# A fused tokenizer, attention and gelu kernel: offset rows by one transfer, a split last group, later preparation, constant products

## The chip, the cores and the metric

The program runs on one core of one Trainium2 chip. The metric is the device time in microseconds of one execution. The core has TensorE (matrix products; it loads the stationary operand first, which the profile counts as PEld), VectorE (DVE), ScalarE (ACT), GpSimd (POOL) and SyncE (SP), which here issues every transfer. Each engine works through its own list of instructions in order; semaphores connect the lists.

## The reference, cut to what matters

Input are 64 images of 3 x 84 x 84 and 64 texts of 77 rows of 192. For each image:

1. Stem: a 4 x 4 convolution with stride 4 to 96 channels on 21 x 21 pixels, batch norm, leaky ReLU.
2. Deformable convolution: a 4 x 4, stride 4 convolution gives 32 offsets (y and x for 16 taps) at 25 positions. Every tap is read bilinearly at its shifted place (zero outside), which makes 96 x 16 values a position; they are multiplied with a 192 x 1536 weight, then bias, batch norm, leaky ReLU: 25 tokens of 192.
3. The 25 tokens and the 77 text rows make 102 rows of 192.
4. Attention: layer norm, integer-rounded q, k, v for 12 heads of 16, scores rounded to 8 bits, an integer softmax (floor, a polynomial for the exponential, a power of two as the result), the weighted sum of v, an output projection, all rounded, plus the residual.
5. Gelu layer: layer norm, 192 to 768 with bias, gelu, 768 to 192, plus the residual. Output is 64 x 102 x 192 in fp32.

## The kernel before, in words

Images are worked in groups of four (GRP), 16 groups in all. The work of a group is cut into named stages, and `SLOT` (lines 66 to 96) is one list of `engine.stage.lag`: in round s the stage works on image s - lag, or, for the stages in `PER_GROUP`, on the whole group. `walk` (line 173) lays the rounds one behind the other, so the order in which an engine meets its stages is written out by hand and repeats each group; up to five groups are under way at a time. `BANKS` (line 101) says which of six PSUM banks a stage's product goes to, and `BankUse` (line 111) makes TensorE wait until the last product of that bank has been read.

The stages that matter here:

- STEM (L1073): the stem as one product for each image; ScalarE's leaky ReLU writes H (L586). HTT (L1081): H transposed in four pieces, copied to HT by ScalarE (L594).
- OFF (L1097), OFS (L1104): the offsets, in four quarters of the partitions, then their sum by `fold`, three copies below one another. ScalarE adds the bias (L609). OFS on GpSimd (`split_offsets`, L523 to L533) splits them into three bf16 parts that sum to the fp32 value, 96 rows in OFFS.
- RX on GpSimd (`mask_offsets`, L544), once an image: the 96 rows are multiplied with a mask that keeps each offset only in the columns of its own tap; with three constant rows this is the right operand, 99 rows of 400 columns (16 taps x 25 positions).
- HAT on TensorE (L1113, L1115): two products with constant lines, the distance of every pixel of a strip from every sampling place in x and y. ScalarE takes absolute values (L618, L622), VectorE turns them into hat functions (HAT, L852) and multiplies x with y (HATW, L858). INT (L1125 to L1129): the interpolation as a product of HT with these weights, copied by ScalarE to SAMP (L629). SD: three transfers pack 96 channels x 16 taps into 128 rows x 12.
- DCN (L1141, L1143): the token product of a group. ScalarE's leaky ReLU writes TOKB (L636); SP stores it (line 481) and loads it back beside the text (LA, line 433).
- LS1, LN1, VE1, RS1, LN1X: statistics, variance, inverse root (GpSimd, L562) and normalised rows XH (L892); TensorE transposes them (L1153), ScalarE copies them to XT (L641). V and FQ: v and q, k. QKC: casts on VectorE (L907 to L911). QD: twelve transfers place the queries of the heads (line 460). SC: scores (L1208, L1211), scaled by ScalarE (L680), clipped by VectorE (L917).
- MAX, MXB, MXC: the row maximum on VectorE (L924 to L934); MAX on GpSimd: the distance from it (L554). BND, QQ, QQG, REM, EP, EXP, SUM, RCP: the integer exponential and its sum on VectorE (L940 to L989); SQ, LOG, PR on ScalarE: square, ten logarithms (L694) and the ratio (L702). PW, PR on VectorE: the power of two (L999, L1006). PT: a transposing transfer. PV2, PV3: weighted sum of v and projection (L1222, L1232). RES: residual (L1025).
- LS2, LN2, VE2, RS2, LN2X: the second layer norm, the same way, into XT2. FFN0, FFN1, FFN2 (`rows_192`, L1174, L1178): two of the six 128-row blocks of the gelu layer each, 408 columns for four images; ScalarE's gelu writes GE (L718), between two loads of its function tables (L572). FF2 (L1247): an image's output product, all in bank 2; VectorE adds the residual (L1032) and frees the bank. YO: two stores a group.
- PREP0 to PREP3: weight preparation on VectorE, once, on the first group: batch norm folded into the tap weights WD (L768 to L772), scalars and rounded qkv weights (L776 to L817, L824, L825), projection weights (L829 to L843). `sampling_constants` (L755) comes before all of them.

What sets the order around the change: before, on VectorE PREP0 and PREP1 stand in front of the first HAT, PREP2 and PREP3 behind the last HATW; on TensorE a steady round runs OFS, FFN0 to FFN2, DCN, HAT 0, FF2 0, FF2 1, HAT 1, FF2 2, PV2, STEM0, LN1X 0, FF2 3, LN1X 1, PV3, LN1X 2, PV2, LN1X 3, V0, FQ0 and so on, with one HTT of the round behind it.

## Time and profile before

| | |
|---|---|
| Runs, median (lowest to highest) | 1056.89 us (1053.66 to 1061.37), 3 runs |
| The profiled execution | 1055.49 us, span from first to last instruction 1053.7 us |
| Busy: TensorE, weight loads | 885.7 us (84%), 539.3 us (51%) |
| Busy: VectorE, ScalarE, GpSimd | 883.3 us (84%), 793.0 us (75%), 301.2 us (29%) |
| Mean granted TensorE clock | 0.950 of full speed |
| Transfers | 53.23 MB, 51 GB/s over the span |

How to read it: busy times are unions, so two instructions that overlap count once. An engine's idle time in front of an instruction is put down to what ended it ("<-"), where that can be inferred. 2.4 GHz is TensorE's full clock; the throttle may grant half of it. The chain of waits that ended last changes engines every microsecond or two; no line of it has over 1.4% of the span beside 4.7% of "issue".

### The profile page before, as it was taken

What the parts mean: (1) busy time and instruction counts of PE and PEld (TensorE: products, weight loads), DVE (VectorE), ACT (ScalarE), POOL (GpSimd) and SP (SyncE); (2) the same over time, 40 slices, a digit from 0 to 9 for tenths busy, and PEclk for the clock granted to TensorE, in tenths of its full rate; (3) what the DMA queues carried; (4) which work ended last, traced back from release to release, by engine and by line L of the source; (5) the groups of instructions that cost most, each with busy time, mean ns of one, the idle gap of its engine ahead of it and who ended that gap; (6) DMA issues with size and microseconds to landing.
All of it is one profiled execution on the core that took longest, in us unless ns stands there. A gap on an engine that the chain in (4) does not pass through costs nothing. (4 is left out here: it accounts for less than half of the span.)

```text
span 1053.7 us, 18633 instructions
## 1 busy us (share of the span) xinstructions
PE 885.7 (84%) x5570; PEld 539.3 (51%) x5570; DVE 883.3 (84%) x1887; ACT 793.0 (75%) x1841; POOL 301.2 (29%) x243
## 2 busy tenths in 40 slices
PE   3769489898989899898989898998989897876737
PEld 2335345555555555555465555555555656454424
DVE  3956988989899898989898998989898989985850
ACT  1435777969697978879696979889796969675742
POOL 5020506042241505051332415050513324130300
PEclk9978779999999999999999999999999999996768
DMA  6010221313122222313121212223141312123020
GB/s 171 22 34 7 59 44 44 63 34 70 41 57 33 65 50 55 60 33 79 37 65 40 64 32 65 50 54 61 33 79 36 65 34 56 32 52 68 11 52 12
DMA packets 131342, 53.23 MB, mean 51 GB/s; under 512 B 103814, under 2 KB 130124, under 8 KB 131148
## 3 DMA queue, kind: packets, MB, share of 16 engines
q1 hardware_dynamic: 131244, 52.05, 23.0%
q8 instruction: 46, 0.75, 0.3%
q14 instruction: 52, 0.43, 0.1%
HBM read 19.84 MB, written 6.24 MB: 25 GB/s over the span
## 5 line engine op out<-in xcount | busy, mean ns | idle before, releaser
L554 POOL TENSOR_TENSOR m_sb<-mx_sb,a_sb 128x1020 f16<-128x1020 f16 x64 | 147.5, 2305 | 192.1 <-DVE mx_sb L934 192.1
L694 ACT ACTIVATE ee_sb<-ee_sb,rs_sb 128x102 f32<-128x102 f32 x640 | 180.1, 379 | 2.8 <-DVE rs_sb L989 2.5
L1247 PE MATMUL bank<-w_out_sb,ge_sb 128*102 128x192 f32 x768 | 144.6, 340 | 37.9 <-DVE y_sb L1032 30.0
L562 POOL TENSOR_TENSOR rstd_sb<-ve_sb,half_sb 102x4 f32<-102x4 f32 x32 | 34.5, 1080 | 445.7 <-DVE ve_sb L885 445.7
L1247 PEld LDWEIGHTS bank<-w_out_sb,ge_sb 128*102 128x102 f32 x768 | 125.8, 175 | 55.0 <-issue 50.3
L1129 PE MATMUL bank<-hats_sb,ht_sb 127*96 127x400 f32 (+1 forms) x384 | 145.1, 514 | 5.4 <-DVE hats_sb L858 5.4
L858 DVE TENSOR_TENSOR hats_sb<-hats_sb 126x1600 f32<-126x1600 f32 x64 | 116.0, 1813 | 0.2
L622 ACT ACTIVATE hats_sb<-bank 126x400 f32<-126x400 f32 (+1 forms) x256 | 107.5, 510 | 0.4 <-PE bank L1115 0.3
L680 ACT ACTIVATE a_sb<-scores,sc_sb 128x1020 f16<-128x1020 f32 x64 | 71.0, 1110 | 39.4 <-POOL m_sb L554 29.7
L1129 PEld LDWEIGHTS bank<-hats_sb,ht_sb 127*96 127x96 f32 (+1 forms) x384 | 59.1, 164 | 72.8 <-issue 64.3
L1174 PE MATMUL bank<-xt_sb,w_in_sb 128*128 128x408 f32 x192 | 84.7, 553 | 8.3 <-ACT ge_sb L718 7.6
L544 POOL TENSOR_TENSOR rx_sb<-offs_sb,mask_sb 96x400 bf16<-96x400 bf16 x64 | 78.8, 1241 | 42.0 <-PE bank L1115 40.6
L1153 PE MATMUL bank<-ident_sb,xh_sb 102*128 102x102 f32 x256 | 51.5, 286 | 46.6 <-ACT xt_sb L641 23.5
L976 DVE SCALAR_TENSOR_TENSOR ee_sb<-sq_sb,sc_sb,ep_sb 128x1020 f32<-128x1020 f32 x64 | 83.3, 1302 | 2.4 <-ACT sq_sb L687 1.2
L641 ACT ACTIVATE xt_sb<-bank 128x204 f32<-128x204 f32 x128 | 43.3, 338 | 49.7 <-PE bank L1153 48.3
L687 ACT ACTIVATE sq_sb<-rm_sb,sc_sb 128x1020 f32<-128x1020 f16 x64 | 73.8, 1154 | 7.0 <-DVE rm_sb L961 7.0
L984 DVE TENSOR_REDUCE ss_sb<-ee_sb 128x10 f32<-128x1020 f32 x64 | 77.2, 1206 | 0.0
L852 DVE TENSOR_SCALAR hats_sb<-hats_sb 126x2000 f32<-126x2000 f32 x64 | 76.5, 1196 | 0.7 <-ACT hats_sb L622 0.7
L1153 PEld LDWEIGHTS bank<-ident_sb,xh_sb 102*128 102x128 f32 x256 | 28.4, 149 | 82.4 <-DVE xh_sb L892 66.2
L1143 PE MATMUL bank<-wdcn_sb,samp_sb 128*100 128x192 f32 x384 | 69.6, 340 | 0.0
L702 ACT ACTIVATE rr_sb<-ee_sb 128x1020 uint16<-128x1020 f32 x64 | 67.2, 1051 | 0.6
L1143 PEld LDWEIGHTS bank<-wdcn_sb,samp_sb 128*100 128x100 f32 x384 | 63.9, 174 | 4.6 <-issue 4.0
(165 smaller groups left out, 1794.9 us busy)
## 6 DMA issues: line engine op xcount, KB each, us to landing
xc_sb<-x_col SPq DMA_DIRECT2D x32, 165.4 KB, 3.1
out<-y_sb SPq DMA_DIRECT2D x32, 153.0 KB
xa_sb<-txt SPq DMA_DIRECT2D x16, 231.0 KB
xr_sb<-txt SPq DMA_DIRECT2D x16, 231.0 KB
q_sb<-qb_sb SPq DMA_DIRECT2D x192, 12.8 KB, 1.9
samp_sb<-samp_sb SPq DMA_DIRECT2D x48, 50.0 KB, 1.9
tok_scratch<-tokb_sb SPq DMA_DIRECT2D x16, 75.0 KB
xa_sb<-tok_scratch SPq DMA_DIRECT2D x16, 75.0 KB
```

Source lines behind the costliest of these rows:

```text
L544: nc.gpsimd.tensor_tensor(RX[b][0:3 * NOFF, :, :], OFFS[:, t.i, :].unsqueeze(1).to_broadcast([3 * NOFF, TAPS, POS]), mask[:].unsqueeze(2). ...
L554: nc.gpsimd.tensor_tensor(M16[b][:], MX[b][:].unsqueeze(2).to_broadcast([128, RT, TOK]), A16[b][:], ALU.subtract).then_inc(m_done, 1)
L622: nc.scalar.activation(HATS[t.i][0:rows, 1 + j, :], bank[t.banks[1]][0:rows, 0:SMP], ACT.Abs, bias=float(-line)).then_inc(ay_done, 1)
L694: last = nc.scalar.activation(EE[b][:, r, :], EE[b][:, r, :], ACT.Ln, scale=RS[b][:, r:r + 1])
L858: v.tensor_tensor(hat[:, 1:, :], hat[:, 1:, :], hat[:, 0:1, :].to_broadcast([rows, NCH, SMP]), ALU.mult).then_inc(w_done, 1)
L976: v.scalar_tensor_tensor(EE[b][:].rearrange("p h k -> p (h k)"), SQ[:], sc[:, CC:CC + 1], EP[:].bitcast(bf16), ALU.add, ALU.mult).then_inc ...
L984: v.tensor_reduce(SS[b][:], EE[b][:], AX.X, ALU.add).then_inc(ss_done, 1)
L1129: last = mm(dst, HT[0:rows, t.i, j, :], HATS[t.i][0:rows, 1 + j, :], start=(j == 0 and not odd), stop=(j == NCH - 2 and odd == 1))
L1143: last = mm(dst, SAMP[:, k, :, :].rearrange("c g p -> c (g p)"), WD[:, k, :], start=False, stop=(k == PACKED - 1))
L1153: last = nc.tensor.transpose(bank[t.banks[0]][:, c * TOK:(c + 1) * TOK], xh[b][:, 64 * c:64 * c + 128], ident[0:TOK, 0:TOK])
L1174: mm(bank[t.banks[c]][:, 0:GRP * TOK], weights(k + c, c), src[:, c, :], start=True, stop=False)
L1247: last = mm(bank[t.banks[0]][0:TOK, 0:D], GE[:, f, t.i * TOK:(t.i + 1) * TOK], WOUT[:, f, :], start=(f == 0), stop=(f == FT - 1))
```

## The change

- Offset rows: RX becomes 9 rows x 16 taps x 4 images x 25 positions, two of them for two groups. Three rows are constant, the six others are the parts of y and x; one transfer of SP a group (`spread_offsets`, stage RP) lays the 96 rows of OFFS into them, tap beside tap. The masks, their constants and `mask_offsets` go. `fold`'s columns are reordered for it, by a copy on VectorE.
- Preparation: PREP1 to PREP3 now stand behind the first group's HAT and HATW on VectorE; the multiplication of the tap weights goes from PREP0 to GpSimd (WDF), behind its first split. The four scalar loads count to the later group of loads.
- Last group: FFA makes the six blocks for the first two images (204 columns each, four banks), FFN0 to FFN2 those for the other two. Moments, variance and inverse root of that group come in pairs too (LN2A, RS2A). Gelu's tables are loaded twice.
- Constant products: `warm` multiplies a constant square with itself, 18 times before and 12 times after the first product; KW00 to KW04 (group 0) and KW10 to KW12 (last group) are four squares each at set places of TensorE's order.
- The whole of SLOT is new, and so are most BANKS. Lags of one engine count from another zero than before, which has no meaning in itself. TensorE's round now runs OFF, LN2X 3, FFA, SC 3, FFN0, OFS, FFN1, FFN2, DCN, HAT 0, FF2 0, FF2 1, HAT 1, PV2 0, STEM0, FF2 2, LN1X 0, HTT 3, PV3 0, LN1X 1, FF2 3, LN1X 2, PV2 1, LN1X 3, V0, FQ0, FQ1, STEM1, HAT 2, INT 0, PV2 2, PV3 1, HTT 0, HAT 3, INT 1, PV3, PV2, INT 2, HTT 1, PV3, SC 0, INT 3, SC 1, LN2X 0, V1, HTT 2, LN2X 1, SC 2, LN2X 2.

```diff
-BANKS = dict(STEM0=(3, 5), STEM1=(1, 4), HTT=(3,), OFF=(3,), OFS=(2,), HAT=(4, 5), INT=(2, 4),
-             DCN=(2,), LN1X=(4,), LN2X=(1,), V0=(0, 3), V1=(5, 0), FQ0=(4, 1), FQ1=(2, 5), PV2=(1,),
-             PV3=(0,), FFN0=(1, 5), FFN1=(4, 3), FFN2=(0, 5), FF2=(2,))
+BANKS = dict(KW00=(1,), KW01=(4,), KW02=(0,), KW03=(1,), KW04=(1,), KW10=(4,), KW11=(4,), KW12=(0,),
+             FFA=(5, 2, 1, 0), STEM0=(3, 2), STEM1=(1, 4), HTT=(4,), OFF=(5,), OFS=(2,), HAT=(5, 0),
+             INT=(3, 1), DCN=(5,), LN1X=(3,), LN2X=(2,), V0=(0, 2), V1=(3, 5), FQ0=(3, 4),
+             FQ1=(0, 5), PV2=(5,), PV3=(0,), FFN0=(1, 5), FFN1=(4, 3), FFN2=(0, 2), FF2=(1,))
...
+            def spread_offsets(t):
+
+                b = t.n % 2
+                sp.wait_ge(part_s, t.count(4, 4))
+                if t.n >= 2:
+                    sp.wait_ge(dy_full, t.count(GRP, -GRP))
+                sp.dma_start(RX[b][3:OFF_ROWS, :, :, :].rearrange("r k g p -> r k (g p)"),
+                             OFFS[:].rearrange("o g p -> o (g p)")).then_inc(rx_in, 16)
...
+            def fold_taps(t):
+                if t.n < 1:
+                    pool.wait_ge(prep, BN2_STEPS)
+                    nc.gpsimd.tensor_tensor(WD[:], WD[:], inv2.unsqueeze(1).to_broadcast([128, PACKED, D]),
+                                            ALU.mult).then_inc(wd_ready, 1)
...
-            def mask_offsets(t):
-
-                b = t.i % 2
...
-                nc.gpsimd.tensor_tensor(RX[b][0:3 * NOFF, :, :],
-                                        OFFS[:, t.i, :].unsqueeze(1).to_broadcast([3 * NOFF, TAPS, POS]),
-                                        mask[:].unsqueeze(2).to_broadcast([3 * NOFF, TAPS, POS]),
-                                        ALU.mult).then_inc(rx_done, 1)
...
+            def warm(dst, square, count):
+
+                for _ in range(count):
+                    last = mm(dst[:, 0:128], square[:], square[:], start=True, stop=True)
+                return last
...
+            warm(bank[1], onesq, 18)
             pe.wait_ge(diag_s, 1)
...
+            warm(bank[1], onesq, 12)
             pe.wait_ge(prep, W1_STEPS)
...
+            def keep_clock(t, end, k):
+
+                if t.n == (LAST_GROUP if end else 0):
+                    free.take(t, 0, warm_s[end][k], 0, 0)
+                    warm(bank[t.banks[0]], ident, 4).then_inc(warm_s[end][k], 1)
...
-                pe.wait_ge(rx_done, t.count(1, 1))
-                rhs = RX[b][:].rearrange("o k p -> o (k p)")
+                pe.wait_ge(rx_in, t.of_group(16, 16))
+                rhs = RX[t.n // GRP % 2][:, :, t.i, :]
...
+            def ffn_in_first_pair(t):
+
+                if t.n == LAST_GROUP:
+                    pe.wait_ge(xt2_done, t.count(GRP, 2))
+                    for f in range(0, FT, 2):
+                        rows_192(t, f, w_in_of, XT2[:, :, 0:2, :].rearrange("p c g q -> p c (g q)"),
+                                 f1_full, ge_done, f % 4)
...
             def ffn_out(t):
-                pe.wait_ge(ge_done, t.of_group(6, 6))
+                pe.wait_ge(ge_done, t.of_group(6, 12 if t.n >= IMG - 2 else 6))
```

## Rows read from the trace of the kernel before

**Rows 1.** Busy us (count) of each engine in a stretch, granted clock, transfers:
```profile
527.00:585.00 58.00, 52.84 (x351) 32.48 (x350) 53.40 (x115) 49.25 (x116) 18.49 (x15) 1.00 0.24 53
```
**Rows 2.** Timeline of VectorE: start us, length us, engine, line, operation, idle before:
```profile
533.93 0.36 DVE L1032 TENSOR_TENSOR y_sb<-bank,x_sb 102x192 f32<-102x192 f32 x1 [0.76 <-PE bank L1247]
...
591.77 0.36 DVE L1032 TENSOR_TENSOR y_sb<-bank,x_sb 102x192 f32<-102x192 f32 x1 [0.76 <-PE bank L1247]
```
**Rows 3.** Waits of TensorE from 411 to 643: us in total, times, longest:
```profile
PE bank L1247 <- DVE y_sb L1032: 6.8, 8, 1.2
PE bank L1153 <- ACT xt_sb L641: 6.4, 12, 0.7
...
PE bank L1174 <- ACT ge_sb L718: 2.2, 4, 0.8
```
**Rows 4.** Timeline of TensorE around the output products:
```profile
582.12 0.95 PE L1174 MATMUL bank<-xt_sb,w_in_sb 128*128 128x408 f32 x2 [0.67 <-ACT ge_sb L718]
...
589.56 2.17 PE L1247 MATMUL bank<-w_out_sb,ge_sb 128*102 128x192 f32 x12 [0.34 <-ACT tokb_sb L636]
592.27 2.17 PE L1247 MATMUL bank<-w_out_sb,ge_sb 128*102 128x192 f32 x12 [0.54 <-DVE y_sb L1032]
...
595.95 2.17 PE L1247 MATMUL bank<-w_out_sb,ge_sb 128*102 128x192 f32 x12 [1.17 <-DVE y_sb L1032]
...
598.36 1.77 PE L1073 MATMUL bank<-xc_sb,stem_w_sb 49*96 49x441 f32 x4
600.65 0.39 PE L1153 MATMUL bank<-ident_sb,xh_sb 102*128 102x102 f32 x2 [0.53 <-DVE xh_sb L892]
...
603.67 0.36 PE L1153 MATMUL bank<-ident_sb,xh_sb 102*128 102x102 f32 x2 [0.67 <-ACT xt_sb L641]
```
**Rows 5.** Waits of VectorE from 411 to 643:
```profile
DVE m_sb L940 <- POOL m_sb L554: 7.1, 4, 1.8
```
**Rows 6.** Single lines over the whole run: count, duration in ns (min/median/max):
```profile
L544 POOL TENSOR_TENSOR rx_sb<-offs_sb,mask_sb x64: 848/1297/1727, 25.2 to 884.7; 96x400 bf16<-96x400 bf16 x64
...
L917 DVE TENSOR_SCALAR a_sb<-a_sb x64: 411/428/1747, 99.5 to 983.9; 128x1020 f16<-128x1020 f16 x64
...
L523 POOL TENSOR_TENSOR offp_sb<-offt_sb,later_sb x16: 350/398/2648, 21.0 to 874.4; 96x100 bf16<-96x100 f32 x16
```
**Rows 7.** Timeline of ScalarE, the logarithms in front of the token copy:
```profile
528.56 2.81 ACT L694 ACTIVATE ee_sb<-ee_sb,rs_sb 128x102 f32<-128x102 f32 x10
```
**Rows 8.** Transfers by line: count, KB each, median us from issue to landing:
```profile
q_sb<-qb_sb SPq DMA_DIRECT2D x192, 12.8 KB, 1.9
```
**Rows 9.** Busy us of each engine in two stretches of the start:
```profile
24.80:37.00 12.20, 7.31 (x14) 2.62 (x14) 11.12 (x32) 7.72 (x18) 3.60 (x5) 1.00 0.29 97
37.00:49.80 12.80, 9.45 (x31) 4.62 (x31) 11.97 (x10) 3.94 (x10) 0.00 (x0) 1.00 0.00 1
```
**Rows 10.** Timeline of the start, all engines:
```profile
26.13 0.56 PE L1113 MATMUL bank<-rx_sb,lx_sb 99*126 99x400 bf16 x1 [5.60 <-DVE sc_sb L782]
...
27.13 1.69 ACT L622 ACTIVATE hats_sb<-bank 126x400 f32<-126x400 f32 x4
...
29.39 0.39 PEld L1073 LDWEIGHTS bank<-xc_sb,stem_w_sb 49*96 49x96 f32 x2 [0.34 <-DMA xc_sb<-x_col]
...
37.05 1.20 DVE L852 TENSOR_SCALAR hats_sb<-hats_sb 126x2000 f32<-126x2000 f32 x1
...
40.17 4.14 PE L1129 MATMUL bank<-hats_sb,ht_sb 126*96 126x400 f32 x6 [5.38 <-DVE hats_sb L858]
...
46.02 2.26 PE L1129 MATMUL bank<-hats_sb,ht_sb 127*96 127x400 f32 x6
...
72.19 1.14 DVE L871 BATCH_NORM_STATS2 st_sb<-xa_sb 102x6 f32<-102x192 f32 x4 [10.13 <-DMA xa_sb<-tok_scratch]
```
**Rows 11.** Timeline of the end:
```profile
1022.28 1.01 POOL L562 TENSOR_TENSOR rstd_sb<-ve_sb,half_sb 102x4 f32<-102x4 f32 x1 [26.80 <-DVE ve_sb L885]
...
1039.60 2.20 PE L1247 MATMUL bank<-w_out_sb,ge_sb 128*102 128x192 f32 x12 [1.18 <-ACT ge_sb L718]
```

215 lines of the change are left out of this document (129 added, 86 removed).

## The prediction

> **What bounds the kernel now.** I read first the busy time of a steady stretch [rows 1]: in 58 us TensorE is busy 52.84, VectorE 53.40, ScalarE 49.25, GpSimd 18.49. No engine is full, two are close to it, so the time is made of busy time plus waits between engines. One group of four images takes the distance of two equal instructions: VectorE's first output addition stands at 533.93 and 591.77 [rows 2], 57.84 apart. Sixteen groups make some 925 of the 1053.7 us; the rest is the way in and the way out.
>
> Which engine closes the period is read from the idle time in front of TensorE's instructions [rows 3, 4]. Over four periods TensorE waited 6.8 us for additions that free the last product's bank, 6.4 for ScalarE to copy transposes, 2.2 for gelu to free a bank; with 0.53 a period for normalised rows, 0.34 for ScalarE's copy of the tokens and some 0.2 of other it is 5.0 a period: 52.84 + 5.0 = 57.84, exactly the period. These waits lie in one short stretch, from the end of the token product to the projection of v (589 to 606); from there TensorE runs without a break until gelu's 0.67 at 582. So the loop is: TensorE's long stretch, then an exchange FF2, addition, normalisation, transpose with VectorE. VectorE has 4.4 us of slack in a period; its largest wait, 1.8 a period for the distance from the maximum [rows 5], costs time only where it makes an addition late.
>
> **Offset rows by transfer.** GpSimd loses the four mask multiplications of a group, 1.30 us each by the median [rows 6], 5.2 us. GpSimd is 32% busy, so its own time is worth nothing. What it does to others is seen in VectorE's clip: 0.428 us by the median, 1.747 at worst [rows 6]. GpSimd stood beside the long ones. The Trainium skill, "GPSIMD Engine Reference", section "Key points", says that GpSimd shares its memory interfaces with VectorE and contends with its two-port modes and its two-input instructions; the spread of the clip agrees. By it GpSimd's remaining work, which is the larger part, still contends. I count 1 us of VectorE's time a period as freed, nothing of it directly on TensorE's loop; bounds 0 and 1.4. One transfer of 19 KB (96 rows of 100 values of 2 bytes) replaces the masks. Transfers of 12.8 KB took 1.9 us [rows 8]; the new one starts after GpSimd's split and is wanted only behind FFN1, FFN2 and DCN, over 8 us of TensorE's work, so it is hidden. Its place on SP is behind the patch loads, queries, packed samples and residual loads; behind it wait the token store and the loads that feed the first layer norm. It waits for the split, which ends before the token product does, so it holds up nobody: cost 0. The two distance products read 9 rows instead of 99; their columns stay 400, so I take no change.
>
> **The new order and banks.** This touches every period, and I price it by the waits of [rows 4]:
> - FF2: the second product still stands right behind the first: 0.54 stays. The third now stands behind the second's hats product, PV2 and the stem (1.77), so the 1.17 goes. The fourth stands after LN1X of image 1, and on VectorE its predecessor's addition after two normalisations, EP and REM: a new wait of 0.7. Sum 1.2 where 1.7 was.
> - Transposes: LN1X of image 0 comes a product later (0.53 becomes 0); images 1 and 2 have HTT, PV3 or FF2 in front of them (0.67 each becomes 0.1), image 3 keeps 0.4. Sum 0.6 where 2.2 was.
> - gelu: FFN2 uses banks 0 and 2, not 5, which FFN0 had: 0.55 becomes 0.
> - Tokens: DCN and the first hats product now share bank 5. Before, the hats product covered part of the wait of 0.34 in front of FF2; now it waits itself: 0.9.
> - Other: three interpolations come before the scores and need VectorE's weights sooner: 0.5 where 0.2 was.
> Sum 3.2, period 52.84 + 3.2 = 56.0; every order leaves some coincidence that such a sum does not see, and I take 56.4: 1.4 us gained, 15 times, **21 us**. Bounds: all waits come back elsewhere (57.84, nothing), or only the 0.54, the 0.9 and half of the rest stay (55.2, 40 us).
>
> **The start.** VectorE's first hats wait behind the scalar and weight preparation (11.12 busy in 24.8 to 37) until 37.05; then hats (to 49.8), then the remaining preparation (to 62.06, where 10.13 us of idling for the tokens begin) until 72.19 [rows 9, 10]. Now the hats come first. But the preparation is not gone: 12.8 of hats and 12.2 + 12.2 of preparation make 37.2 in a row before the first layer norm. They start when the offset rows have landed and a hat is made of them, 2.7 us from the first distance product (26.13) to ScalarE's last of four (27.13 and 1.69) [rows 10]. Without the long split step and the mask (2.3 and 0.85) the rows would be split at about 23; I allow up to 24, for three transposes now ahead of the offset products. The transfer takes 1.9, or it stands behind the weight loads, behind which the second patches became usable only at 29.39 [rows 10]. That gives 27.6 to 32 for the first hat and 65 to 69 for the layer norm, plus up to 3 for stems that ScalarE does before the third hat. I take 70: **2 us gained**, bounds 0 and 6. The token product, 9 us earlier, gains nothing alone: VectorE is late in its place. The tap weights' multiplication moves to GpSimd: 2304 columns by the 0.848 for 400 are 4.9 us, behind the first split, 20 us ahead of DCN: 0; and the split's first step no longer runs beside it (2.648 at worst, 0.398 by the median [rows 6]), which the chain gets back and the transfer spends.
>
> **Constant products.** A fp32 product of 400 columns took 0.69 us per instruction at 40 and 0.377 at 46 [rows 10]; the granted clock in between rose to 2.4 GHz. A 128-column square is thus 0.44 or 0.24 us, 18 of them 7.9 or 4.3, before the first real product, which was due at 5.6. They delay it by 0 to 3.5 and may halve the first stems (1.8 us each): 0 in sum, bounds -2 and +3. The Trainium skill, "TensorE: Matmul & The Clock Gate", section "The HAM clock gate", says that sustained work brings the full rate and idling takes it back. By it the squares help the stems only, since the wait for the first offsets is not filled. The steady stretch is at full clock already [rows 1]. Of the eight groups of four squares three stand among full periods: 1 us each, of which I take **2 us lost**.
>
> **The end.** The last group's chain went VectorE, GpSimd 1.01 at 1022.28, normalisation, transposes, FFN, last gelu, 1.18 us of TensorE idle, FF2 at 1039.60 [rows 11]. Statistics of the first pair are now ready earlier, but its transposes and its FFN stand behind the second pair's on VectorE and TensorE; so what is saved is the wait for gelu (1.18) and part of the 1.01 for GpSimd. Four squares between the first two transposes cost 1 to 1.8. Two more table loads lie under TensorE's products. **1 us gained**, bounds -3 and +4.
>
> **Sum.** 1055.5 (the profiled execution: span 1053.7 and 1.8 around it; 1.4 below the median of 1056.9) - 21 - 2 + 2 - 1 = 1033.5. I forecast **1034**.
>
> **Rivals.**
> 1. *Waits all go* (chance 0.18). TensorE's period is 55.2: 1055.5 - 40 - 1 = about 1015. For it: VectorE has slack of 4 us and GpSimd is freed. Against: FF2 and additions still alternate on one bank.
> 2. *Waits only move* (0.19). The new order gives each wait a new owner, period 57.6 to 57.9; start, end and squares leave 1050 to 1055. For it: both busy engines leave under 5 us a period, and the old order had reached that too. Here the change does at the ends what it says and nothing in the middle.
> 3. *Slower: the token copy* (0.10). DCN and the next hats product share bank 5, and ScalarE's copy of the tokens stands behind ten logarithms, 2.81 us [rows 7], that need VectorE's reciprocal. If these start only when DCN ends, TensorE waits 3.1 instead of 0.34: period 56.4 + 2.2 = 58.6, +0.8 x 15, about 1068 with the ends. It decides from a wait of 2.3 us. Against: the old order has the same logarithms in front of the same copy, and TensorE waited 0.34 for it [rows 4].
> 4. *Forecast* (0.53): 1034, from 1022 to 1044.
>
> **The numbers.** The range takes the forecast, half of rival 1 and most of rival 2: 1016 to 1053. Within 1% is what a measurement of this kernel can hardly tell from no change, 1046.3 to 1067.5. Faster by over 1%: 0.53 + 0.18 + 0.02 of rival 2 = 0.73. Same: 0.18. Slower: 0.09, where rival 3 goes past its price.
>
> **What would show it.** Distance of equal additions: 56.4, not 57.8. No idle of 1.2 before the third FF2, 0.7 before the fourth; bank 5 wait under 1.5 before the hats product. GpSimd busy 230 us, VectorE's clip as before in the worst case. First layer norm near 70, with VectorE busy right up to it. If the additions are 57.8 apart with other waits, rival 2; if ScalarE's token copy is named in front of the hats product with over 2 us, rival 3. The forecast is wrong most easily in the 1.4 us a period.

## The result, and the profile after

| | before | changed |
|---|---|---|
| Median of 18 runs (lowest to highest) | 1057.14 us (1053.33 to 1064.6) | 1063.74 us (1054.45 to 1070.61) |
| Ratio, changed to before | | 1.0049, 95% interval 1.0029 to 1.007 |
| Profiled execution (its span) | 1055.49 (1053.7) us | 1057.11 (1055.3) us |
| Busy, whole run: TensorE, VectorE, ScalarE, GpSimd | 885.7, 883.3, 793.0, 301.2 us | 896.0, 906.5, 798.3, 217.6 us |
| First y addition of group 0, of group 13, of group 15, end | 183.8, 939.8, 1041.8, 1053.7 | 181.6, 944.4, 1043.4, 1055.3 |

The change makes the kernel half a per cent slower; 1034 was forecast. The last row of the table, taken from VectorE's additions (L1032 before, L1084 now), says where: 2.2 us gained before the first of them, 6.8 lost in the 13 periods that follow, 3.0 gained in the last two, 1.6 lost in sum. The 21 us expected of the middle are missing altogether. The profiled execution of the changed kernel is among its fastest, 6.6 us under its median, that of the kernel before 1.65 under its own; so the two traces show 1.6 us of a loss of 5 (by the ratio) to 6.6 us (by the medians).

The steady stretch again, busy time by engine as in [rows 1], here in three neighbouring stretches of the changed kernel:

```profile
469.00:527.00 58.00, 53.31 (x351) 33.84 (x350) 54.85 (x113) 49.23 (x116) 12.71 (x10) 0.97 0.27 53
527.00:585.00 58.00, 51.48 (x350) 32.29 (x349) 55.02 (x115) 49.35 (x117) 12.72 (x10) 1.00 0.27 53
585.00:643.00 58.00, 53.32 (x351) 33.79 (x350) 54.91 (x114) 49.40 (x117) 12.72 (x10) 0.97 0.29 53
```

GpSimd fell from 18.49 to 12.7, as forecast. VectorE was to lose 1 us of its 53.40 and gained 1.6. TensorE reads 51.48 at full clock and 53.3 where the clock fell for a moment, and yet the additions stand 57.8 to 58.1 apart in all three: TensorE's amount of work does not set the distance. At full clock it is also less than before, by 1.2 us over one period, first the kernel before, then the changed one:

```profile
533.93:591.77 57.84, 52.67 (x348) 32.32 (x348) 53.23 (x114) 49.09 (x116) 18.33 (x15) 1.00 0.24 52
534.04:591.87 57.83, 51.46 (x348) 32.28 (x348) 54.76 (x114) 49.19 (x116) 12.72 (x10) 1.00 0.27 52
```

So TensorE idles 6.4 us in that period where it idled 5.2.

The additions that answer to [rows 2], VectorE's timeline:

```profile
534.04 0.36 DVE L1084 TENSOR_TENSOR y_sb<-bank,x_sb 102x192 f32<-102x192 f32 x1 [0.87 <-DMA out<-y_sb]
...
591.87 0.36 DVE L1084 TENSOR_TENSOR y_sb<-bank,x_sb 102x192 f32<-102x192 f32 x1 [1.05 <-DMA out<-y_sb]
```

57.83 apart, where 57.84 was. What ended the wait in front of them is new: not TensorE, but the store of the output rows of the group before. All waits of TensorE and VectorE over the four periods from 411 to 643, answering to [rows 3] and [rows 5] (us in total, times, longest):

```profile
PE bank L1332 <- DVE y_sb L1084: 8.5, 4, 2.2
PE bank L1184 <- ACT tokb_sb L660: 4.2, 4, 1.1
DVE y_sb L1084 <- DMA out<-y_sb: 4.1, 4, 1.2
PE bank L1295 <- DMA pt_sb<-p_sb: 3.9, 4, 1.2
PE bank L1225 <- ACT xt_sb L665: 3.2, 5, 1.8
```

TensorE's waits are 2.1 + 1.05 + 1.0 + 0.8 and 0.05 of others a period: 5.0, the same sum as before, under other names. That is a mean over four periods: 6.2 where the clock stays full, 4.4 to 4.9 where it falls. The wait for gelu and the one of 1.17 before the third output product are gone, as forecast. In their place stand one of 2.1 before the second output product and one of 1.0 for the transposed probabilities, of which the forecast knew nothing.

Why the store is late is seen on SyncE. Timeline around one exchange, several engines:

```profile
582.25 0.83 SPq L492 DMA_DIRECT2D rx_sb<-offs_sb  x1
...
584.43 2.81 ACT L718 ACTIVATE ee_sb<-ee_sb,rs_sb 128x102 f32<-128x102 f32 x10
...
587.15 0.31 ACT L660 ACTIVATE tokb_sb<-bank 100x192 f32<-100x192 f32 x1
587.49 0.29 SPq L498 DMA_DIRECT2D tok_scratch<-tokb_sb  x1
...
587.83 0.30 SPq L504 DMA_DIRECT2D out<-y_sb  x1
...
592.37 2.17 PE L1332 MATMUL bank<-w_out_sb,ge_sb 128*102 128x192 f32 x12 [2.09 <-DVE y_sb L1084]
```

The first output store of a group (L504) has had its rows since the exchange of the period before. In the new order it stands on SyncE behind the token store (L498), which waits for ScalarE's copy (L660), behind ten logarithms. It is issued at 587.83; only when it has landed may VectorE overwrite the rows, at 591.87, some 4 us later, and TensorE's second output product waits 2.09 for that. In the kernel before, the same store left right behind the exchange, 47 us ahead of the addition at 591.77:

```profile
544.46 0.60 SPq L487 DMA_DIRECT2D out<-y_sb  x1
```

VectorE's own growth sits in two lines. Count and duration in ns (min/median/max) over the run, answering to [rows 6], and GpSimd's distance from the maximum:

```profile
L969 DVE TENSOR_SCALAR a_sb<-a_sb x64: 414/421/2051, 101.3 to 990.8; 128x1020 f16<-128x1020 f16 x64
...
L1020 DVE TENSOR_SCALAR ep_sb<-qq_sb x64: 413/421/2119, 107.9 to 1007.5; 128x1020 int16<-128x1020 int16 x64
...
L564 POOL TENSOR_TENSOR m_sb<-mx_sb,a_sb x64: 1884/1891/2937, 103.1 to 1002.5; 128x1020 f16<-128x1020 f16 x64
```

The clip (L969) and the power bits (L1020) take 0.42 alone. Three times a period one of them starts beside GpSimd's distance of 1.89 and takes 1.8 to 2.1 (over the run 25 clips of 64 take 0.97 or more, with a median of 2.04, and 15 power bits of 64 take 2.1).

The start, answering to [rows 10]; timeline of GpSimd, SyncE, TensorE and VectorE:

```profile
23.44 0.37 POOL L556 TENSOR_TENSOR offs_sb<-offr_sb,offp_sb 96x100 bf16<-96x100 f32 x1
...
23.84 0.86 SPq L492 DMA_DIRECT2D rx_sb<-offs_sb  x1
...
30.25 0.56 PE L1184 MATMUL bank<-rx_sb,lx_sb 9*126 9x400 bf16 x1 [7.71 <-issue]
...
33.07 1.20 DVE L891 TENSOR_SCALAR hats_sb<-hats_sb 126x2000 f32<-126x2000 f32 x1 [9.05 <-ACT hats_sb L646]
...
72.76 1.14 DVE L922 BATCH_NORM_STATS2 st_sb<-xa_sb 102x6 f32<-102x192 f32 x4
```

The rows were split at 23.81 and of use at 30.25: 6.4 us for a transfer priced at 1.9, while the weight and patch loads of the start were under way (333 GB/s from 22.5 to 27.7, 281 to 30.2). VectorE idles 9.05 for the first hats, and the first layer norm starts at 72.76, 0.57 later than before, now without a wait in front of it.

### The profile page after: what moved, and what is told of

It reads as the page before. It is cut to its first block and busy times, and to the rows that moved or that the text cites. A ratio compares the mean times of both kernels' runs of the same rounds, so it can differ in the third digit from the quotient of the medians.

```text
span 1055.3 us, 18850 instructions
## 1 busy us (share of the span) xinstructions
PE 896.0 (85%) x5718; PEld 566.4 (54%) x5718; DVE 906.5 (86%) x1887; ACT 798.3 (76%) x1849; POOL 217.6 (21%) x181
## 5 line engine op out<-in xcount | busy, mean ns | idle before, releaser
L1332 PE MATMUL bank<-w_out_sb,ge_sb 128*102 128x192 f32 x768 | 155.4, 357 | 38.4 <-DVE y_sb L1084 37.2
L564 POOL TENSOR_TENSOR m_sb<-mx_sb,a_sb 128x1020 f16<-128x1020 f16 x64 | 128.3, 2005 | 267.1 <-DVE mx_sb L986 267.1
L718 ACT ACTIVATE ee_sb<-ee_sb,rs_sb 128x102 f32<-128x102 f32 x640 | 180.1, 378 | 1.6 <-DVE rs_sb L1041 1.2
L1332 PEld LDWEIGHTS bank<-w_out_sb,ge_sb 128*102 128x102 f32 x768 | 132.9, 184 | 60.5 <-issue 56.0
L573 POOL TENSOR_TENSOR rstd_sb<-ve_sb,half_sb 102x4 f32<-102x4 f32 (+1 forms) x33 | 38.1, 1154 | 455.4 <-DVE ve_sb L937 455.4
L1200 PEld LDWEIGHTS bank<-hats_sb,ht_sb 127*96 127x96 f32 (+1 forms) x384 | 58.2, 164 | 71.5 <-issue 69.4
L1028 DVE SCALAR_TENSOR_TENSOR ee_sb<-sq_sb,sc_sb,ep_sb 128x1020 f32<-128x1020 f32 x64 | 81.6, 1275 | 4.0 <-ACT sq_sb L711 2.3
L1247 PE MATMUL bank<-xt_sb,w_in_sb 128*128 128x408 f32 (+1 forms) x204 | 82.7, 530 | 0.0
L969 DVE TENSOR_SCALAR a_sb<-a_sb 128x1020 f16<-128x1020 f16 x64 | 61.9, 968 | 13.3 <-ACT a_sb L704 13.2
L665 ACT ACTIVATE xt_sb<-bank 128x204 f32<-128x204 f32 x128 | 43.7, 342 | 36.5 <-PE bank L1225 36.3
L740 ACT ACTIVATE ge_sb<-bank,b_in_sb 128x408 f32<-128x408 f32 (+1 forms) x102 | 53.4, 577 | 11.9 <-PE bank L1251 10.9
## 6 DMA issues: line engine op xcount, KB each, us to landing
q_sb<-qb_sb SPq DMA_DIRECT2D x192, 12.8 KB, 1.9
```

The costliest lines, as they stand in the source:

```text
L564: nc.gpsimd.tensor_tensor(M16[b][:], MX[b][:].unsqueeze(2).to_broadcast([128, RT, TOK]), A16[b][:], ALU.subtract).then_inc(m_done, 1)
L718: last = nc.scalar.activation(EE[b][:, r, :], EE[b][:, r, :], ACT.Ln, scale=RS[b][:, r:r + 1])
L1028: v.scalar_tensor_tensor(EE[b][:].rearrange("p h k -> p (h k)"), SQ[:], sc[:, CC:CC + 1], EP[:].bitcast(bf16), ALU.add, ALU.mult).then_inc ...
L1200: last = mm(dst, HT[0:rows, t.i, j, :], HATS[t.i][0:rows, 1 + j, :], start=(j == 0 and not odd), stop=(j == NCH - 2 and odd == 1))
L1247: mm(bank[t.banks[first + c]][:, 0:n], weights(k + c, c), src[:, c, :], start=True, stop=False)
L1332: last = mm(bank[t.banks[0]][0:TOK, 0:D], GE[:, f, t.i * TOK:(t.i + 1) * TOK], WOUT[:, f, :], start=(f == 0), stop=(f == FT - 1))
```

## The experiments

All ratios are to the kernel before, on the same chip. "Store-first" is the changed kernel with the mend of the first experiment.

**e1_store_first.** Edit, in the list of the order:

```diff
-dve.PREP0.0 ... act.SQ.12 dve.HATW.92 sp.DCN.8
+dve.PREP0.0 ... act.SQ.12 dve.HATW.92
-dve.SC.99 ... sp.YO0.20 dve.MAX.99 ...
+dve.SC.99 ... sp.YO0.20 sp.DCN.8 dve.MAX.99 ...
```

> The changed kernel with one entry moved: SyncE issues the first output store of a group (YO0) ahead of the store of the tokens (DCN), not behind it. In the changed kernel VectorE's first output addition waits 0.9 to 1.05 us in each group for that store, which is issued at 587.8 though its rows are ready 57 us earlier, and TensorE's second output product waits 2.2 us behind it. Theory A, SyncE's queue closes the loop: both waits fall (the first to 0, the second to about 1.2), the distance of equal additions goes from 58.0 to about 57.0, and the time is about 15 us under that of the changed kernel, near 1049 (ratio to the kernel before about 0.992). Theory B, VectorE (busy 55.0 of 58.0, with short waits of many kinds) and ScalarE close it: the wait for the store goes, another wait of VectorE or TensorE takes its place, the distance stays 57.7 to 58.1, and the ratio to the kernel before stays at 1.002 to 1.007.

Measured: 1042.27 us, ratio 0.9884 (0.9846 to 0.9922), intervals apart from the changed kernel's. VectorE's additions, no wait left in front of them, 56.73 apart (57.0 to 57.4 in most periods):

```profile
526.70 0.35 DVE L1084 TENSOR_TENSOR y_sb<-bank,x_sb 102x192 f32<-102x192 f32 x1
...
583.43 0.35 DVE L1084 TENSOR_TENSOR y_sb<-bank,x_sb 102x192 f32<-102x192 f32 x1
```

Theory A holds, and the gain is larger than its 0.992, which still lies inside the interval: one entry in SyncE's queue cost 1.65%, more than the whole change lost. The steady period fell by about 0.8 us, which makes 12 us of the 17; the two traces differ by 15.1 over the 13 periods, since long ones are fewer too.

**e2_old_order.** The changed code with the order and the banks of before, the last group in one piece, no constant products; the list against that of before:

```diff
-... pool.RX.5 ... pool.RX.4 ... pool.OFS.0 ... pool.RX.3 ... sp.LR.12 ... pool.RX.2 ...
+... pool.OFS.0 pool.WDF.0 ... sp.LR.12 sp.RP.4 ...
```

> The offset rows by one transfer a group and the tap weights' product on GpSimd, but the order of all engines and the banks of the kernel before, the last group in one piece and no constant products. Theory A, the new order brought nothing and the transfer nothing: within 0.2% of the kernel before, period 57.8 to 58.0, VectorE's clip as before. Theory B, GpSimd freed of the masks makes VectorE faster, as forecast: VectorE busy 52.4 a period where 53.4 was, period up to 1 us less, 1042 to 1050. Theory C, GpSimd's distance from the maximum, once it no longer waits behind masks, stands beside VectorE's two-port operations: VectorE busy 54.5 to 55 a period, period 58.2 or more, ratio 1.003 to 1.010. In the changed kernel VectorE's busy time of a period rose from 53.4 to 55.0; A and B put that on the new order, C on the masks' going.

Measured: 1060.31 us, 1.0051 (1.002 to 1.0082). Busy time by engine in the steady stretch:

```profile
527.00:585.00 58.00, 53.26 (x350) 32.25 (x348) 52.62 (x115) 49.19 (x116) 13.32 (x11) 1.00 0.25 53
```

A new wait of TensorE, over four periods:

```profile
PE bank L1176 <- DMA rx_sb<-offs_sb: 3.4, 4, 0.9
```

VectorE is at 51.9 to 52.7 in five neighbouring stretches, 53.0 to 53.4 before, so the masks' going did free some 0.9 of the 1 us forecast, and theory C falls: it is the new order that put VectorE up. The time did not follow: the steady period stayed at 57.9, with 0.85 for the landing of the rows in the place of older waits. Nor does the steady period show the half per cent that this kernel is slower; in its trace the first addition comes 3.0 us later than before, and one late period takes 62.3.

**e8_old_order_split_first.** In e2's list `pool.OFS.0` moved ahead of `pool.MAX.9`.

> The old order with the transfer (ratio 1.005), and GpSimd's split of the offsets ahead of the distance of the third image, not behind it. There the rows are split at 531.2 and land at about 534, TensorE waits 0.88 for them before the first hats product of each group, though ScalarE's offsets are ready at 524.06. Theory E, the transfer's latency is what the old order pays: the wait goes, period 57.0, ratio 0.992 to 0.995. Theory F, in the old order the waits only move (the loop is closed elsewhere): wait gone, period still 57.8, ratio 1.000 to 1.006. If so, transfer and masks are worth nothing by themselves.

Measured: 1064.51 us, 1.0065 (1.0041 to 1.009). The wait for the rows is gone, TensorE waits 0.6 for the token copy and as long as before for transposes instead, and the steady period is 57.9: theory F. In the old order this wait only moved.

**e3_no_squares.** All constant products taken out.

```diff
-            warm(bank[1], onesq, 18)
-            warm(bank[1], onesq, 12)
-WARM = 5, 3
+WARM = 0, 0
```

> The changed kernel without any of its constant products (the 30 at the start and the 8 groups of four). By the forecast's step they cost 2 us: about 1062, 0.998 of the changed kernel. If they cost nothing that ends last: the same as the changed kernel within 1 us. Rival, they are worth something: the first stems and the products before the first offset rows take 2 to 3 us longer at the lower clock, first normalised rows later than 75.7, and the time is 2 to 4 us above the changed kernel (ratio to the kernel before 1.007 to 1.009).

Measured: 1056.93 us, 1.0018 (0.9995 to 1.0042), some 3 us less than with them by the ratios; the intervals overlap, so that it is clear neither of nothing nor of the forecast's 2. The products do halve the stems (0.98 for the first pair, 1.79 before), but these start 2.3 us later behind them (9.11 without), and the offset sum 1.6 later (19.72 without). The first addition stands only 0.6 us earlier without them, so where the rest of the 3 us lies is not shown. TensorE's timeline of the changed kernel:

```profile
11.44 0.98 PE L1136 MATMUL bank<-xc_sb,stem_w_sb 49*96 49x441 f32 x4
...
21.29 0.34 PE L1175 MATMUL bank<-offq_sb,fold_sb 128*96 128x100 f32 x2
```

**e4_one_piece.** The conditions on the last group set to never true for the layer norm and gelu layer (`PAIRS = -1`).

> The changed kernel with the last group's second layer norm and gelu layer in one piece, as before (four images, no FFA). By the forecast's step the split is worth 1 us: about 1064.7. Theory of this run: from the last group's first output addition to the end the changed kernel takes 11.9 us (1043.4 to 1055.3) and the kernel before 11.9 (1041.8 to 1053.7), but the distance of the last two first additions fell from 45.9 to 42.8, and if that is the split, then without it the end comes 3 us later: 1066 to 1067. Rival: the split costs, by its second pair of table loads (1.28 us each) and its narrower products, and without it the time is 1 to 2 us lower.

Measured: 1064.39 us, 1.0086 (1.0054 to 1.0119). By the ratios the split is worth 0.37%, some 4 us, but the intervals overlap, and 1 us is not ruled out. In the traces the last two distances between first additions sum to 102.3 in one piece, 99.0 split, 102.0 before; among the other kernels with the split that sum goes from 98.0 (e3) to 104.9 (e1), so one trace does not settle it either.

**e5_distance_on_vector.** On store-first:

```diff
-                nc.gpsimd.tensor_tensor(M16[b][:], MX[b][:].unsqueeze(2).to_broadcast([128, RT, TOK]),
+                v.tensor_tensor(M16[b][:], MX[b][:].unsqueeze(2).to_broadcast([128, RT, TOK]),
                                 A16[b][:], ALU.subtract).then_inc(m_done, 1)
```

> The store-first kernel with the distance from the maximum computed by VectorE, right behind the last maximum, and no more by GpSimd. In the store-first kernel VectorE is busy 55 to 55.7 us in 58; its clip of 0.43 takes 1.77 and 2.06, its power bits 2.11 instead of 0.42, each time next to GpSimd's distance of 1.9, some 4.9 us a period over the shortest durations. Theory C, the two engines are in each other's way, and VectorE is now the bound: the four distances cost VectorE 4 x 0.69 = 2.8 (the row of the remainder, same kind and size) and the clip and power bits are back at 0.42 in every instance; VectorE busy about 2 us less a period, the waits for GpSimd go, period 55 to 56.3 where 57.1 was, ratio to the kernel before 0.955 to 0.977. Theory D, the long ones are not GpSimd's doing (their place, or their data, makes them long): they stay, VectorE gets 2.8 us more, period 58.5 or more, ratio over 1.005.

Measured: 1059.22 us, 1.0037 (1.0019 to 1.0056). The clip over the whole run of this kernel, and then VectorE's groups by shape from 411 to 643 (busy, mean ns, idle before):

```profile
L962 DVE TENSOR_SCALAR a_sb<-a_sb x64: 364/421/536, 100.0 to 991.5; 128x1020 f16<-128x1020 f16 x64
```

```profile
L986 DVE TENSOR_TENSOR m_sb<-mx_sb,a_sb 128x1020 f16<-128x1020 f16 x16 | 19.5, 1221 | 0.5
...
L1021 DVE TENSOR_SCALAR ep_sb<-qq_sb 128x1020 int16<-128x1020 int16 x16 | 6.7, 419 | 0.0
```

The mechanism of theory C is shown: with no distance on GpSimd, no clip takes over 0.54 and the power bits 0.42 on average. The price of theory C was wrong: the distance costs VectorE 1.22, not 0.69, since one operand is broadcast. Four of them are 4.9 us, as much as the interference had cost: VectorE is busy 55.1 us a period here and 54.7 in e1. In VectorE's time GpSimd's help with the distance is worth next to nothing. In the kernel's time it is worth 1.5%: the period is 58.5, where e1 has 57.0 to 57.4. What VectorE's 0.4 us do not explain of that is not shown.

**e6_sums_behind, e11_maxima_behind_exp, e12_both.** VectorE's softmax in other orders, on store-first. e6: `MXC1 EXP0 SUM0 RCP0 SC2 ... MXC2 EXP1 SUM1 RCP1 SC3`. e11: `SC2 MAX2 EXP0 MXC1 SUM0 RCP0 ... SC3 MAX3 EXP1 MXC2 SUM1 RCP1`, and ScalarE's SC3 behind FFN1, SQ1 behind FFN2. e12: e11 with DCN in bank 4.

> The store-first kernel with VectorE's order changed within the softmax: remainder and power bits of images 0 and 1 ahead of the next image's last maximum, and exponential, sum and reciprocal behind it, ahead of the next clip; so an fp32 exponential (1.28) and sum (1.21) stand beside GpSimd's distance of images 1 and 2 (1.9 each), not a 16-bit clip or power bits. Theory C, 16-bit one-input operations wait for GpSimd and these do not: two of the three long instances of a period (1.6 too long each) go back to 0.42, VectorE busy about 3 us less a period, period 56 or a little under if no wait takes their place, ratio 0.965 to 0.98. Theory D, what stands beside GpSimd is slowed whatever it is: VectorE's busy time as in the store-first kernel, ratio 0.986 to 0.992. Third outcome: exponentials now wait for ScalarE's square, VectorE less busy but more idle, ratio 0.985 or above.

> The store-first kernel with VectorE's softmax in another order: the last maxima of images 1 and 2, which release GpSimd's distance, stand behind the exponential of the image before, so that the sum (1.21, a reduction) stands beside the distance, as it already does in the last image, where neither is slowed. The ordering tried before put the exponential beside it, and that took 10.4 us too long in four periods. ScalarE's scaling of the fourth scores goes behind FFN1's gelu and its second square behind FFN2's, since the distance comes some 4 us later. Theory C: clip and power bits of images 1 and 2 are back at 0.42, the clip of image 1 stays long; VectorE's busy time of a period falls from 54.8 to 51.5 to 52.5, period 55.5 to 56.5, ratio 0.964 to 0.98. Rival: VectorE is less busy, but its softmax now waits for ScalarE's squares and GpSimd's distance in a row, period 57 to 59, ratio 0.987 to 1.01.

> Both changes of the two kernels before it: token product in bank 4, last maxima behind the exponential. If theory C holds (VectorE busy 2.5 us less) and TensorE's exchange is the next in line, the bank gives another 0.5 to 1 us a period over the new softmax order alone: 0.955 to 0.97. If the bank is worth nothing in either order, the same as the new softmax order within 0.2%.

Measured: 1090.24 us, 1.0301 (1.0275 to 1.0326); 1083.26 us, 1.0244 (1.0212 to 1.0276); 1094.34 us, 1.0336 (1.0295 to 1.0377). In e6 the exponential, which theory C had keep its time, was the one held up (31 of 64, 2.5 by the median), L1028 over the run:

```profile
L1028 DVE SCALAR_TENSOR_TENSOR ee_sb<-sq_sb,sc_sb,ep_sb x64: 1270/1282/2833, 108.6 to 1045.8; 128x1020 f32<-128x1020 f32 x64
```

In e11 VectorE was less busy (51.4 to 53.4 in 58), but waited 9.6 us in four periods for ScalarE's squares and TensorE 8.3 for the token copy, and periods of 58.6 and 60.6 took turns: the rival. In e11 longer waits in the chain cost more than the interference did. The token bank on top (e12) made it slower again, not faster.

**e7_store_first_no_squares.**

> The store-first kernel without any constant products. In the order of the changed kernel they cost about 3 us (ratio 1.0018 without, 1.0049 with). If they delay the start alone, the same is saved here: ratio 0.985 to 0.987. If the saving was in the period through TensorE's clock, it is saved or not whatever the order: the granted clock of the run then is above 0.94.

Measured: 1042.35 us, 0.9868 (0.9839 to 0.9898). It lies under e1's 0.9884 by half of what e3 saved, but within the intervals; not told apart. The granted clock is higher, 0.938 to 0.949 where e1 has 0.927 to 0.939, but most of that is no gain: the trace of e1 counts 17 us at half rate ahead of 43.7, that of e7 has no entry of the clock ahead of 43.4 and counts that time as full.

**e9_prep_first, e14_scalars_first.** On e7. e9: `dve.PREP1.92` back to `dve.PREP1.0`, behind PREP0. e14:

```diff
                 then(v.tensor_tensor(dcnb[:], dcnb[:], bm2[:, 0, :], ALU.add))
+                scalars()
...
             def qkv_integers():
-                scalars()
```

> The store-first kernel without constant products (ratio 0.9868), and the scalars and the rounding of the qkv weights (PREP1) back in front of VectorE's first hats, where they stood before; the projection weights stay behind the hats. In the changed kernel VectorE idles 9.05 us at 33.07 for the first hats (the offset rows, split at 23.81, reach TensorE at 30.22, 6.4 us later, not 1.9), then 22.6 us of preparation follow the hats and the first layer norm starts at 72.76, with VectorE busy up to it. Theory G, this idle time is what the new place of the preparation wasted: with 12.2 us of it ahead of the hats these start near 37, the preparation behind them is 10 us shorter, first layer norm at 64 to 69 (or when the tokens have landed), everything after it 4 to 8 us earlier, ratio 0.979 to 0.983. Rival: the tokens now land near 72 as before (the token product and its round trip close the start), VectorE idles there instead, ratio 0.985 to 0.989.

> The store-first kernel without constant products, and of the preparation only the scalars (5.9 us of small operations, 50.18 to 56.03 in the changed kernel) in front of the first hats, where VectorE idles 9.05; all the rest stays behind them. With the whole preparation behind the hats VectorE reaches the first layer norm at 72.76 and the tokens (issued 66.15) have long landed; with PREP1 in front the hats start near 37 and the tokens land at 72.2. Theory: both ends count, and this takes 5.9 off VectorE's and nothing from the tokens': first layer norm when the tokens land, 69.4 to 70, 3 us earlier, ratio 0.983 to 0.985. Rival: the 3 us are lost again before the second group (q and k, low granted clock of TensorE from 67 to 84), ratio 0.986 to 0.988.

Measured: e9 1043.48 us, 0.9866 (0.983 to 0.9902), its rival; e14 1039.13 us, 0.9825 (0.9784 to 0.9866), as its theory has it, though its interval overlaps that of e7. VectorE's first layer norm in e9:

```profile
72.20 1.14 DVE L921 BATCH_NORM_STATS2 st_sb<-xa_sb 102x6 f32<-102x192 f32 x4 [8.51 <-DMA xa_sb<-tok_scratch]
```

and in e14:

```profile
69.71 1.14 DVE L921 BATCH_NORM_STATS2 st_sb<-xa_sb 102x6 f32<-102x192 f32 x4 [2.55 <-DMA xa_sb<-tok_scratch]
```

Two ends close the start: VectorE's preparation and the landing of the tokens. All of the preparation behind the hats makes VectorE the later one (72.76), 12 us of it in front makes the tokens late (72.20, 8.51 idle). The 5.9 us that fit in the idle time bring the first layer norm 3 us forward, as expected, and the first addition of group 0 stands at 177.4, after 180.3 in e7. That second number scatters: it is 175.4 to 180.1 in the four kernels with the scalars first, 180.0 to 182.2 in e1, e7 and e15 without.

**e10_token_bank.** On store-first, `DCN=(5,)` to `DCN=(4,)`.

> The store-first kernel with the token product in bank 4 and not in bank 5, which it shares with the next hats product. There TensorE waits 1.11 in each group for ScalarE's copy of the tokens, behind ten logarithms (rival 3 of the prediction). Theory H, TensorE's exchange closes the loop of 57.1: the wait goes, the period falls to 56.0 to 56.4, ratio 0.972 to 0.978. Theory I, VectorE (54.8 busy of 57.1) closes it: the wait goes and comes back in front of the second output product and the transposes, period 57.0 to 57.3, ratio 0.986 to 0.990.

Measured: 1051.06 us, 0.9926 (0.9898 to 0.9955), slower than store-first if anything. TensorE's waits over four periods:

```profile
PE bank L1332 <- DVE y_sb L1084: 7.6, 4, 2.4
PE bank L1295 <- DMA pt_sb<-p_sb: 4.5, 3, 2.1
```

The wait for the token copy is gone and the one before the second output product is back (1.9 a period for store-first's 1.0). Periods of 57.1 to 57.9 and of 58.3 to 58.5 take turns. Neither theory had it slower.

**e13_no_clip.** On e7, the clip left out, the first maximum waiting for the scores themselves.

> The store-first kernel without constant products (ratio 0.9868), with VectorE's clip of the scores left out, nothing else (so out-of-range scores are not limited; what is computed differs in that). The four clips take 0.42, 1.77, 0.41 and 2.06 of VectorE in a period, 4.7 in sum; part of the two long ones will pass to whatever then stands beside GpSimd's distance. Theory I, VectorE closes the loop of 57.1: the period falls by at least the four short ones, 1.7, to 53.5 to 55.4, ratio 0.93 to 0.962. Theory H', TensorE (52.2 to 52.6 busy) or ScalarE (50.3) closes it by its exchanges: the period stays above 56.5, ratio 0.978 or more.

Measured: 1042.44 us, 0.9845 (0.9793 to 0.9897), period 57.0 to 57.2. Busy time in the steady stretch, and then VectorE's greatest wait over four periods:

```profile
527.00:585.00 58.00, 53.37 (x350) 33.69 (x348) 52.88 (x110) 50.05 (x119) 13.19 (x11) 0.97 0.27 54
```

```profile
DVE m_sb L990 <- POOL m_sb L563: 7.4, 4, 1.9
```

Theory I falls: VectorE does 2.8 us less in 58 (55.7 in e14) and nothing comes of it. It waits 1.85 a period for GpSimd's distance instead, 0.4 more than in e14 for ScalarE's squares and 0.3 more for the inverse root.

**e15_two_inputs_beside, e16_combined.** On e7: `... QQG0 SC2 MXC1 REM0 MAX2 EP0 ...`; e16 with e14's scalars too.

> The store-first kernel without constant products, with three of VectorE's softmax steps moved: the third image's clip ahead of the second's last maximum, and behind that maximum the remainder (0.68, two inputs) and the third image's first maximum (0.43, two inputs), then the power bits, which stood second beside the distance and took 2.11. In the runs so far the operations with two 16-bit inputs and the reductions kept their time beside the distance, those with one input waited for its end. Expected by that: power bits 1.2 to 1.5 instead of 2.11, VectorE busy 0.6 to 0.9 less a period, period 56.3 to 56.6, ratio 0.975 to 0.982. Rival: as in the two orders tried before, a wait for ScalarE's square takes its place, period 57.1 or more, ratio 0.987 or above.

> The two changes before together: scalars in front of the first hats, and the moved softmax steps. If both hold, 3 us from the start and 0.6 us from each of 15 periods over the store-first kernel without constant products: ratio 0.971 to 0.979. If the softmax steps give nothing, as the scalars alone, 0.983 to 0.985.

Measured: 1040.69 us, 0.9832 (0.979 to 0.9874) and 1040.25 us, 0.9842 (0.9798 to 0.9887), told apart neither from e7 and e14 nor from each other. Most of e15's steady periods are 57.0 to 57.5 again, not 56.3 to 56.6; in e16's trace 57.2 to 57.4 and 58.3 to 58.8 mix. The power bits are at 0.42 in every instance, but the first maximum took their place, though it has two inputs; e15 over the run:

```profile
L975 DVE TENSOR_TENSOR ma_sb<-a_sb x64: 410/422/2117, 100.5 to 978.0; 128x520 f16<-128x520 f16 x64
...
L1019 DVE TENSOR_SCALAR ep_sb<-qq_sb x64: 408/417/425, 109.2 to 991.0; 128x1020 int16<-128x1020 int16 x64
```

**e17_second_bank, e18_early_p.** On e14. e17:

```diff
-LN1X=(3,)
+LN1X=(3, 5, 3, 3)
-bank[t.banks[0]]
+bank[t.banks[t.i % len(t.banks)]]
```

e18 also moves `dve.PW.99 dve.PR.99` to behind `dve.SUM.98`.

> The kernel with the scalars first (ratio 0.9825, period 57.0 to 57.1), with the first layer norm's second transpose in bank 5 and no more in bank 3 behind the first one. There the second transpose starts at 590.82 after an idle time of 1.57, right after ScalarE's copy of the first at 590.31, which stands behind ten logarithms (587.60, 2.84), while its rows were ready at 588.9. Theory J, the loop of 57.1 is TensorE's work plus its exchange waits: this wait falls from 1.57 (or 1.8) to under 0.4, the output product behind it starts 1.4 earlier, period 55.7 to 56.5, ratio 0.958 to 0.973. Theory K, VectorE's and GpSimd's softmax chain closes it in time, whatever their amount of work: the wait moves to another instruction of TensorE, period 56.9 to 57.3, ratio 0.980 to 0.987.

> The kernel before it, and the first image's power of two (both steps) on VectorE ahead of the third image's remainder, the second's reciprocal and the third's power bits: its ratio from ScalarE is there at 578.27, the steps ended at 580.69, the transposing transfer lands some 4.3 later and TensorE waits 1.25 for it. Theory J: 0.7 to 0.9 us a period less than the kernel before, if the later square of the third image does not take it back; ratio 0.01 under that of the kernel before. Theory K: no change, or slower by the later remainder, within 0.3% of it.

Measured: e17 1036.74 us, 0.9811 (0.9774 to 0.9847); e18 1044.35 us, 0.9887 (0.9848 to 0.9926). TensorE's timeline in e17:

```profile
586.33 0.34 PE L1223 MATMUL bank<-ident_sb,xh_sb 102*128 102x102 f32 x2
587.90 2.17 PE L1330 MATMUL bank<-w_out_sb,ge_sb 128*102 128x192 f32 x12 [1.23 <-DVE y_sb L1083]
```

The second transpose no longer waits, and the output product behind it waits 1.23 instead: theory K, period 57.0 to 57.4. e18 falls outside both theories: it is 0.8% slower than e17, the intervals just apart, and TensorE waits 2.2 us a period for additions where e17 has 1.7; why is not shown. e17 is the fastest version, 1.9% under the kernel before and 2.4% under the changed one by the two ratios; against e14 alone its interval overlaps.

## Why the prediction was wrong

**The new order and banks: this step failed.** It foresaw 3.2 us of TensorE's waits where 5.0 were, and 5.0 are measured (6.2 in a period at full clock). Right were the third output product (0), gelu (0) and nearly the tokens (0.9, measured 1.05). Wrong were three terms. "FF2: Sum 1.2": measured 2.1, all before the second product, since the sum took the addition as waiting for TensorE alone and never asked what VectorE's write waits for. "Other: 0.5": the probabilities' transfer takes 1.0 by itself. "Transposes 0.6": measured 0.8. The first is settled by e1: with the output store ahead of the token store 1.0 of the 2.1 is left, and the period is some 0.8 us shorter. The forecast did read SyncE's queue, but only for what stands behind the new transfer ("holds up nobody", which is right in the steady stretch, where it leaves at 582.25); the store's new place was in the same list.

The store is not all of it. In e1, where it is mended, TensorE's waits are 5.0 us a period again: 1.0 for the additions, 1.05 for the tokens, 1.5 for transposes and normalised rows (forecast 0.6), 1.4 for the probabilities and others (forecast 0.5). The sum also held TensorE's work at 52.84, and that fell by 1.2 at full clock, which the forecast did not foresee; with the 52.7 of before, waits of 5.0 make a period of 57.7.

**TensorE taken as what closes the loop.** Its sum of work and waits gave 57.84 exactly [rows 1, 3, 4], and that was read as proof. It is none: the idle time of any engine fills its period up. That it came out to the last digit was luck, too, since the 52.84 are those of 58 us, not of the period (52.67). Waits taken away in e8, e10 and e17 came back in front of another instruction, as rival 2 had it ("waits only move", 0.19). Its price, 1050 to 1055, was still too low. (The price of rival 3 adds up to 1066, not 1068; nothing rests on it.)

**VectorE's 1 us.** Right for the masks (e2: 0.9), but the new order set the distance beside the clip and the power bits, 4.8 us a period, reckoned as what VectorE's instructions beside it took over the short ones of their kind. The same reckoning gives 1.2 before, or 2.6 with the instructions that stood beside the distance and a mask or split step. In the forecast GpSimd "stood beside the long ones" of the clip; it did not look at which operations the new order puts beside the distance.

The Trainium skill, "SBUF — State Buffer", section "SBUF: two separate sides", says that the port pair VectorE and GpSimd share is held for a whole instruction by whichever starts first: one of GpSimd's, or one of VectorE's in a two-port mode or with two SBUF inputs. The traces agree: operations of one input (clip 0.42 to 2.05, power bits 0.42 to 2.12, normalised rows 0.38 to 1.88) and those with two (exponential 1.28 to 2.5 in e6, remainder 0.68 to 1.5 before, first maximum 0.42 to 2.12 in e15, second 0.29 to 0.83 in e11) were held up to the end of the distance, while sums and reciprocals kept their time (1.20 to 1.22, 0.20 to 0.22). It goes the other way too: in the kernel before, one distance of each period took 3.4 us while the clip, the remainder and the power bits beside it kept theirs:

```profile
573.80 3.39 POOL L554 TENSOR_TENSOR m_sb<-mx_sb,a_sb 128x1020 f16<-128x1020 f16 x1 [2.49 <-DVE mx_sb L934]
573.93 0.42 DVE L917 TENSOR_SCALAR a_sb<-a_sb 128x1020 f16<-128x1020 f16 x1
```

My expectation of e15, that two 16-bit inputs are not held up, went against the page and was wrong.

**The start** (forecast 2 us, layer norm at 70). The step mis-sized the transfer: 6.4 us from split to use, not 1.9, behind the weight loads; the hats began at 33.07, outside the 27.6 to 32. They took 17.1 instead of 12.8, since VectorE, now earlier, waits 2.4 and 2.6 for ScalarE in between. TensorE did nothing from 22.5 to 30.2 meanwhile and was granted 1.2 GHz from 27.7 to 44.8. That is hardly a loss against before: there a product of 400 columns took 0.69 at 40 and 0.377 at 46 [rows 10], too. The 1.00 of [rows 9] does not say otherwise, for the clock's first entry in that trace stands at 44.0, and what lies ahead of it is counted as full; so the mean clocks of the two traces (0.950, 0.930) cannot be compared either. The layer norm came at 72.76. The 2.2 us that the first addition is ahead all the same were won later: ScalarE's first scaling of scores is still at 100.2, 98.3 before.

**The constant products** (2 us lost): 3 by the ratios of e3, not told apart from 2. The Trainium skill, "TensorE: Matmul & The Clock Gate", section "The HAM clock gate", says that sustained work brings the full rate: the stem pair at 0.98 agrees; nothing shows that it paid, since the stems started 2.3 us later behind the squares.

**The end** (1 us gained): right in sign; 3.0 in the trace and 4 by the ratios of e4, neither of them clear of 1.

**What stays open.** Six versions with the store mended (e1, e7, e13, e14, e15, e17) have most of their steady periods at 57.0 to 57.4. It is not VectorE's amount of work (e13), the token bank (e10) or the transpose's bank (e17), and putting the distance on VectorE makes it 58.5. No run changes ScalarE's order alone, so its part is untested. What fits is a loop of two stretches, argued and not shown: VectorE and GpSimd in turn from the first scores to the third addition, then TensorE from the fourth output product to the next scores. Nor is it shown why, in the changed kernel, single periods of 59 to 61 come in (824 to 944 in its profile). Between 240 and 950 that profile has ten short stretches at 1.2 GHz where the one before has four, nine of them within 7 us behind a group's first addition, in or behind the exchange with its idle TensorE. From 476 to 766 periods with and without one are equally long (57.8 to 58.2); all periods of 59 and more from 240 on have one, which may be cause or consequence.

## What to carry to other kernels

When an order is rewritten, list for every instruction in the critical exchange all that it waits for, the stores that must have left its buffer too, and look up each of their places in the DMA queue: one entry moved was worth 1.65%. A sum of busy time and waits that gives the period exactly holds for every engine and proves nothing of which one closes it; a wait is worth what an experiment gives that removes it, and here three of the four waits removed one by one (e8, e10, e17, not e1) came back elsewhere. Before work is put on GpSimd, ask what VectorE runs beside it: a distance of 1.9 us there cost VectorE 1.3 to 1.7 in three of four cases, in sum as much time as doing it itself. Then ask the whole kernel, not VectorE's busy time: with the distance on VectorE it was 1.5% slower all the same.

## What was not expected of the hardware

A transfer of 18.8 KB was of use 6.4 us after its rows were ready while weight loads were under way, and 4 us in the steady stretch is the time from the issue of an output store to the release of its buffer (587.83 to 591.87). The same fp16 subtraction takes VectorE 0.68 with two plain operands and 1.22 with one of them broadcast along the row (e5), GpSimd 1.89.
